# Four-layer residual network on one core: order of the LoRA spread, split float32r for a weight mix, earlier last products, a store in halves

## The reference

```python
# 0: one expert for each batch element, argmax of cond_8; H = 256
up, gate = x @ wu.T + bu, x @ wg.T + bg;  out = (silu(up) * gate) @ wd.T + bd
# 1: base weight, and LoRA of 8 experts of rank 16, mixed by cond_8
out = x @ W_base.T + b_base + 2.0 * sum_e cond[b, e] * (x @ As[e].T) @ Bs[e].T
# 2: a weight for each batch element, mixed from 8 by cond_8, masked
w_b = sum_g cond[b, g] * (weight[g] * mask);  out = x @ w_b.T + bias
# 3: top-2 of 8 gelu-gated experts with softmax weights, and a shared one; H = 512
out = sum_k w[b, k] * mlp(x, expert[b, k]) + mlp(x, shared)
```

## Time and profile before

| what | us |
|---|---|
| runs, median (3 runs) | 153.5 (153.43 to 153.65) |
| the profiled execution, its own time | 153.69 |
| its span in the profile | 151.7 |
| TensorE busy | 147.4 (97% of the span) |
| VectorE busy | 109.8 (72%) |
| ScalarE busy | 72.0 (47%) |
| GpSimd busy | 91.4 (60%) |

### The profile page before, as it was taken

One profiled execution on the slowest core, in us unless ns is written; L12 is line 12 of the kernel. 1 busy time (PEld: TensorE's weight loads), 2 busy tenths in 40 slices (PEclk: granted clock), 3 DMA queues, 4 the chain that ended last, 5 costly groups with the idle time before them and its releaser, 6 DMA issues.

```text
span 151.7 us, 3108 instructions
## 1 busy us (share of the span) xinstructions
PE 147.4 (97%) x1075; PEld 135.1 (89%) x1075; DVE 109.8 (72%) x229; ACT 72.0 (47%) x138; POOL 91.4 (60%) x93
## 2 busy tenths in 40 slices
PE   7999999999999999999999999999999999999992
PEld 2479999999978999999989999999999999999881
DVE  3985666667996586867775967876587895968772
ACT  2875444461375554454444354545425434345640
POOL 1003999999700007849994939995876999880000
PEclk9999999999999999999999999999999999999999
DMA  2999999974354676393397386095447047000052
GB/s 62 414 401 403 411 405 394 420 298 144 154 190 138 175 160 225 78 302 109 78 309 252 130 269 215 0 300 206 190 134 280 4 139 274 4 4 0 0 209 72
DMA packets 13912, 30.15 MB, mean 199 GB/s; under 512 B 1337, under 2 KB 8009, under 8 KB 13769
## 3 DMA queue, kind: packets, MB, share of 16 engines
q1 hardware_dynamic: 13472, 28.76, 54.7%
q10 hardware_dynamic: 424, 1.20, 2.0%
HBM read 24.71 MB, written 1.05 MB: 170 GB/s over the span
## 4 chain that ended last, share of the span: by engine, by line
PE 89%; DVE 4%; POOL 3%; ACT 2%; issue 1%; ACTq 0%; DVEq 0%; POOLq 0%
PE pair L550 22%; PE pair L540 12%; PE acc L599 10%; PE pair L482 10%; PE pair L557 8%; PE acc L584 6%; PE acc L608 5%; PE acc L490 5%; PE acc L438 2%; PE pair L526 2%; PE pair L497 2%; POOL duo_lo L372 2%; PE pair L471 2%; PE pair L445 2%; DVE hid L771 2%; ACT hid_hi L431 2%
## 5 line engine op out<-in xcount | busy, mean ns | idle before, releaser
L372 POOL TENSOR_TENSOR duo_lo<-raw_duo,duo_hi 128x512 fp32r<-128x512 f32 x36 | 48.6, 1350 | 2.9
L762 DVE TENSOR_TENSOR hid_lo<-hid,hid_hi 128x512 fp32r<-128x512 f32 (+1 forms) x41 | 36.1, 882 | 17.8 <-ACT hid_hi L431 17.3
L431 ACT ACTIVATE hid_hi<-hid 128x512 fp32r<-128x512 f32 (+1 forms) x41 | 25.4, 621 | 44.0 <-DVE hid L771 41.1
L369 POOL CAST duo_hi<-raw_duo 128x512 fp32r<-128x512 f32 x36 | 28.3, 786 | 28.5 <-PE acc L599 28.5
L771 DVE TENSOR_TENSOR hid<-pair,act 128x512 f32<-128x512 f32 (+1 forms) x49 | 32.9, 673 | 5.7 <-PE pair L550 4.2
L550 PE MATMUL pair<-x_duo,duo_hi 128*128 128x256 f32 x192 | 35.2, 281 | 0.2 <-POOL duo_lo L372 0.2
L412 ACT ACTIVATE act<-pair 128x512 f32<-128x512 f32 x48 | 28.3, 590 | 9.7 <-PE pair L550 7.7
L550 PEld LDWEIGHTS pair<-x_duo,duo_hi 128*128 128x128 f32 x192 | 29.7, 189 | 0.8 <-issue 0.3
L550 PE MATMUL pair<-x_duo,duo_lo 128*128 128x256 f32 x96 | 26.9, 280 | 0.0
L540 PE MATMUL pair<-x_hl,shared_hi 128*128 128x512 f32 x64 | 20.5, 401 | 0.1
L550 PEld LDWEIGHTS pair<-x_duo,duo_lo 128*128 128x128 f32 x96 | 18.0, 188 | 0.0
(11 more groups left out here) (101 smaller groups left out, 199.2 us busy)
## 6 DMA issues: line engine op xcount, KB each, us to landing
raw_duo<-experts SPq DMA_DIRECT2D x12, 768.0 KB, 5.2
ring<-experts SPq DMA_DIRECT2D x16, 386.5 KB, 6.7
raw_solo<-experts SPq DMA_DIRECT2D x8, 768.0 KB, 5.3
x_duo<-x_hl SPq DMA_DIRECT2D x24, 128.0 KB, 4.0
x<-xT ACTq DMA_DIRECT2D x1, 1024.0 KB, 6.2
lora_raw<-x SPq DMA_DIRECT2D x4, 256.0 KB, 2.4
raw_solo<-shared SPq DMA_DIRECT2D x1, 768.0 KB, 9.8
out<-lora_raw SPq DMA_DIRECT2D x3, 256.0 KB, 2.8
```

The costliest lines, as they stand in the source:

```text
L369: pool.tensor_copy(duo_hi[:, j % HALVES, piece(n)], raw_duo[:, j % RAWS, piece(n)])\
L372: pool.tensor_tensor(duo_lo[:, j % HALVES, piece(n)], raw_duo[:, j % RAWS, piece(n)], duo_hi[:, j % HALVES, piece(n)].bitcast(F32), ALU.su ...
L431: act.activation(hid_hi[:, k % SPLITS, at], hid3[:, u % PAIRS, at], ACT.Copy)\
L762: dve.tensor_tensor(hid_lo[:, k % SPLITS, at], hid3[:, u % PAIRS, at], hid_hi[:, k % SPLITS, at].bitcast(F32), ALU.subtract).then_inc(hid_ ...
```

## The change

It does five things. SyncE loads `lora_sb` ahead of `cond_sb`. VectorE makes the first piece of `bs_w` ahead of the copy of `at_row`, which in turn stands ahead of `onehot` and `chosen_b`; TensorE makes `prepare1(0)` ahead of the rank products, and two warming products in a row instead of one and two. Layer 2's weight mix is made in float32r from split operands: GpSimd splits `w2_sb` into `w2_hi` and `w2_lo`, two experts at a time, VectorE splits `y_delta` into `y_hi` and `y_lo` right behind it, and TensorE makes three float32r products where there was one in float32; the split parts use buffers that layer 3 needs later. `gateup(47)` is put right behind `gateup(46)`, ahead of `down(44)`. The last store is cut into partitions 0 to 63 on SyncE's queue and 64 to 127 on ScalarE's.

```diff
--- before.py
+++ after.py
@@ -79,6 +79,8 @@
     ORDER += _di[0:2] + _si[0:1] + _ri[0:1] + _di[2:4] + _si[1:2] + _di[4:6] + _ri[1:2] + _si[2:3]
 ORDER += _d[18:20] + _r[6:7] + _d[20:22] + _r[7:8] + _d[22:24] + _s[12:16]
 UNITS = len(ORDER)
+
+LAST = slice(B * P - N2, B * P)
 AT = {unit: n for n, unit in enumerate(ORDER)}
 SPLIT_AT = {unit: n for n, unit in enumerate(x for x in ORDER if x[0] != "R")}
 ENDS = [x for x in ORDER if x[0] == "R" or (x[0] == "D" and x[2] == 1)]
@@ -183,6 +185,9 @@
         lora_raw = sb("lora_raw", [P, B, P])
         x_sum = lora_raw[:, :, :].rearrange("p b n -> p (b n)")
         lin1 = sb("lin1", [P, B, P])
+        w2_hi = duo_hi[:, 0, 0:E * P].rearrange("p (k n) -> p k n", k=E)
+        w2_lo = duo_lo[:, 0, 0:E * P].rearrange("p (k n) -> p k n", k=E)
+        y_hi, y_lo = x_duo[:, 0, 0, :], x_duo[:, 0, 1, :]
         mix_raw = sb("mix_raw", [P, E, B, R])
         lin2 = sb("lin2", [P, B, P])
 
@@ -216,6 +221,8 @@
         chosen_done, rank_mm, payload_done, slots_mm, slots_done = (
             sem("chosen_done"), sem("rank_mm"), sem("payload_done"), sem("slots_mm"), sem("slots_done"))
         ydelta_done, bsw_done = sem("ydelta_done"), sem("bsw_done")
+        yhi_done, ylo_done, w2_hi_done, w2_lo_done = (
+            sem("yhi_done"), sem("ylo_done"), sem("w2_hi_done"), sem("w2_lo_done"))
         prep_mm, prep_copied = sem("prep_mm"), sem("prep_copied")
         lin2_done, lin1_done = sem("lin2_done"), sem("lin1_done")
         shared_hi_done, shared_done = sem("shared_hi_done"), sem("shared_done")
@@ -251,8 +258,8 @@
 
         @block.sync
         def _(sp):
+            sp.dma_start(lora_sb[:, :], lora).then_inc(lora_in, 16)
             sp.dma_start(cond_sb[:, :], cond).then_inc(cond_in, 16)
-            sp.dma_start(lora_sb[:, :], lora).then_inc(lora_in, 16)
             sp.dma_start(w2_sb[:, :, :], w2).then_inc(w2_in, 16)
 
             def load0(b):
@@ -327,11 +334,12 @@
             sp.wait_ge(x_summed, SUMMED[ORDER[-1]] - 2)
             for g in range(G - 1):
                 sp.dma_start(out[:, group(g)], x_sum[:, group(g)]).then_inc(stored, 16)
-            for n in range(2):
-                at = slice((G - 1) * N + n * N2, (G - 1) * N + (n + 1) * N2)
-                sp.wait_ge(x_summed, SUMMED[ORDER[-1]] - 1 + n)
-                sp.dma_start(out[:, at], x_sum[:, at]).then_inc(stored, 16)
-            sp.wait_ge(stored, 16 * (G + 1))
+            at = slice((G - 1) * N, (G - 1) * N + N2)
+            sp.wait_ge(x_summed, SUMMED[ORDER[-1]] - 1)
+            sp.dma_start(out[:, at], x_sum[:, at]).then_inc(stored, 16)
+            sp.wait_ge(x_summed, SUMMED[ORDER[-1]])
+            sp.dma_start(out[0:P // 2, LAST], x_sum[0:P // 2, LAST]).then_inc(stored, 16)
+            sp.wait_ge(stored, 16 * (G + 2))
 
         @block.gpsimd
         def _(pool):
@@ -339,6 +347,14 @@
             pool.memset(ones[:, :], 1.0).then_inc(ones_set, 1)
             pool.wait_ge(cond_in, 16)
             pool.tensor_copy(earlier_b[:, :], cond_sb[:, EARLIER:EARLIER + B]).then_inc(ones_set, 1)
+
+            pool.wait_ge(w2_in, 16)
+            for n in range(E // 2):
+                at = slice(2 * n, 2 * n + 2)
+                pool.tensor_copy(w2_hi[:, at, :], w2_sb[:, at, :]).then_inc(w2_hi_done, 1)
+                pool.wait_ge(w2_hi_done, n + 1)
+                pool.tensor_tensor(w2_lo[:, at, :], w2_sb[:, at, :], w2_hi[:, at, :].bitcast(F32), ALU.subtract)\
+                    .then_inc(w2_lo_done, 1)
 
             pool.wait_ge(small_in, 16)
             pool.wait_ge(slots_done, 1)
@@ -431,6 +447,9 @@
                         act.activation(hid_hi[:, k % SPLITS, at], hid3[:, u % PAIRS, at], ACT.Copy)\
                            .then_inc(hid_hi_done, 1)
 
+            act.wait_ge(x_summed, SUMMED[ORDER[-1]])
+            act.dma_start(out[P // 2:P, LAST], x_sum[P // 2:P, LAST]).then_inc(stored, 16)
+
         @block.tensor
         def _(pe):
             def warm(times):
@@ -452,24 +471,25 @@
             pe.wait_ge(ones_set, 3)
             pe.wait_ge(at_diag_done, 1)
             pe.matmul(acc[1][:, 0:B], ones_b[:, :], at_diag[:, :], start=True, stop=True).then_inc(at_mm, 1)
-            warm(1)
+            warm(2)
+            prepare1(0)
 
             pe.wait_ge(chosen_done, 1)
             pe.matmul(pair[2][0][0:B, 0:E], earlier_b[:, :], chosen_b[:, :], start=True, stop=True)
             pe.matmul(pair[2][0][0:B, E:2 * E], ones_b[:, 0:B], chosen_b[:, :], start=True, stop=True)\
               .then_inc(rank_mm, 1)
-            warm(2)
-            for q in range(G):
+            for q in range(1, G):
                 prepare1(q)
 
-            pe.wait_ge(ydelta_done, 1)
-            pe.wait_ge(w2_in, 16)
+            pe.wait_ge(ylo_done, 1)
             for k in range(E):
                 n = G + k // 2
                 if k % 2 == 0:
                     pe.wait_ge(prep_copied, n - len(prep) + 1)
-                ins = pe.matmul(prep[n % 3][:, (k % 2) * B * R:(k % 2 + 1) * B * R], w2_sb[:, k, :],
-                                y_delta[:, :, :].rearrange("p b j -> p (b j)"), start=True, stop=True)
+                    pe.wait_ge(w2_lo_done, k // 2 + 1)
+                for m, (w, y) in enumerate(((w2_hi, y_hi), (w2_hi, y_lo), (w2_lo, y_hi))):
+                    ins = pe.matmul(prep[n % 3][:, (k % 2) * B * R:(k % 2 + 1) * B * R], w[:, k, :], y,
+                                    start=(m == 0), stop=(m == 2))
                 if k % 2 == 1:
                     ins.then_inc(prep_mm, 1)
 
@@ -617,8 +637,11 @@
             gateup(1)
             pe.wait_ge(lin_read, 2 * G)
             for u in range(UNITS):
-                if u + AHEAD < UNITS:
+                if u + AHEAD < UNITS - 1:
                     gateup(u + AHEAD)
+                if u + AHEAD == UNITS - 2:
+
+                    gateup(UNITS - 1)
                 down(u)
 
         @block.vector
@@ -633,31 +656,40 @@
             dve.tensor_tensor(at_diag[:, :], top_at[:, 0:1].to_broadcast([B, B]), cond_sb[:, EYE:EYE + B], ALU.mult)\
                .then_inc(at_diag_done, 1)
 
-            step = [3]
-
-            def chained(ins):
-                step[0] += 1
-                ins.then_inc(route, 1)
-                dve.wait_ge(route, step[0])
-
-            chained(dve.tensor_tensor(onehot[:, :, :], top_at[:, 0:K].unsqueeze(2).to_broadcast([B, K, E]),
-                                      cond_sb[:, IOTA:IOTA + E].unsqueeze(1).to_broadcast([B, K, E]), ALU.is_equal))
-            dve.tensor_tensor(chosen_b[:, :], onehot[:, 0, :], onehot[:, 1, :], ALU.add).then_inc(chosen_done, 1)
-            dve.wait_ge(rep_in, 16)
-            dve.wait_ge(at_mm, 1)
-            dve.tensor_copy(at_row[:, :], acc[1][0:1, 0:B]).then_inc(at_done, 1)
-            dve.wait_ge(lora_in, 16)
-            for q in range(G):
+            def spread(q):
                 at = slice(q * GB, (q + 1) * GB)
                 dve.scalar_tensor_tensor(
                     bs_w[:, at, :], lora_sb[:, BS1:BS1 + P].unsqueeze(1).to_broadcast([P, GB, P]), LORA_SCALE,
                     cond_rep[:, at].unsqueeze(2).to_broadcast([P, GB, P]), ALU.mult, ALU.mult)\
                    .then_inc(bsw_done, 1)
 
+            dve.wait_ge(rep_in, 16)
+            dve.wait_ge(lora_in, 16)
+            spread(0)
+            dve.wait_ge(at_mm, 1)
+            dve.tensor_copy(at_row[:, :], acc[1][0:1, 0:B]).then_inc(at_done, 1)
+            step = [3]
+
+            def chained(ins):
+                step[0] += 1
+                ins.then_inc(route, 1)
+                dve.wait_ge(route, step[0])
+
+            chained(dve.tensor_tensor(onehot[:, :, :], top_at[:, 0:K].unsqueeze(2).to_broadcast([B, K, E]),
+                                      cond_sb[:, IOTA:IOTA + E].unsqueeze(1).to_broadcast([B, K, E]), ALU.is_equal))
+            dve.tensor_tensor(chosen_b[:, :], onehot[:, 0, :], onehot[:, 1, :], ALU.add).then_inc(chosen_done, 1)
+            for q in range(1, G):
+                spread(q)
+
             dve.wait_ge(small_in, 16)
-            dve.tensor_tensor(y_delta[:, :, :], cond_rep[:, :].unsqueeze(2).to_broadcast([P, B, R]),
-                              small_sb[:, DELTA:DELTA + R].unsqueeze(1).to_broadcast([P, B, R]), ALU.mult)\
+            delta = small_sb[:, DELTA:DELTA + R].unsqueeze(1).to_broadcast([P, B, R])
+            dve.tensor_tensor(y_delta[:, :, :], cond_rep[:, :].unsqueeze(2).to_broadcast([P, B, R]), delta, ALU.mult)\
                .then_inc(ydelta_done, 1)
+            y = y_delta[:, :, :].rearrange("p b j -> p (b j)")
+            dve.wait_ge(ydelta_done, 1)
+            dve.tensor_copy(y_hi, y).then_inc(yhi_done, 1)
+            dve.wait_ge(yhi_done, 1)
+            dve.tensor_tensor(y_lo, y, y_hi.bitcast(F32), ALU.subtract).then_inc(ylo_done, 1)
 
             dve.wait_ge(exp_done, 1)
             chained(dve.reciprocal(inv[:, 0:1], expsum[:, :]))
```

(8 more changed lines are left out.)

5 lines of the change are left out of this document (removed).

## The result

Four runs have a median of **157.35 us** (157.26 to 158.75) against 153.57 us for the kernel before: a ratio of **1.0262**, 95% interval 1.0202 to 1.0323. The forecast was 156.0 us in a range up to 157.2: the sign was right, the size was too small, and the median lies 0.15 us outside the range. (Ratios pair runs of one chip and leave disturbed runs out, so they can differ a little from the quotient of two medians.)

The account below looks back on a forecast made before the run. TensorE bounds the kernel, with VectorE's payload chain setting the head: 153.69 + 2.55 (later slots' product) − 0.05 (last unit) = 156.2, median 0.19 below, so 156.0 us; range 153.9 to 157.2.

Parts of the forecast that it names:

- TensorE has no slack, and the head's delay reaches the end: Whole kernel: TensorE busy 147.4 of 151.7 us, so what the head gains or loses arrives at the end.
- Turns, for 16 partitions too: Head: VectorE's narrow two-operand instructions also wait out GpSimd's; payload at 15.2 to 15.3, L506 2.55 us later; chance 0.60.
- the second rival: Head: only wide instructions take turns with GpSimd; L506 1.65 us later, 155.1 us in all; chance 0.13.
- The first turn: Head: VectorE's `spread(3)` waits for GpSimd's first cast and ends at 6.7 us, ahead of `y_delta`.
- `y_hi` and `y_lo`, 0.75: VectorE's chain in the head: the new copy and subtraction add 0.75 us, between 0.5 and 0.9.
- `cond`, 0.5: Start of VectorE's chain: `cond`, second in the queue, delays all that hangs on it 0.5 us, at most some 0.8.
- TensorE would be at `upgate0(0)` near 11.1: Head: with all inputs ready TensorE reaches `upgate0(0)` near 11.1 instead of 11.94; float32r products save 0.65 us.
- The store, taken as 0: Tail: storing the last piece in halves costs 0 us, between −0.2 and +0.4.
- 0.4 in a rival: Tail: store halves go one behind the other at half rate, 0.9 us instead of 0.45; chance 0.25 within any case.
- The last unit, 0.05: Tail: `gateup(47)` ahead of `down(44)` gains 0.05 us most likely, nothing at least, 0.35 at most.
- The clock falling behind the idle stretch: Layer 0: 2 us idle ahead of L506 drops the clock to 1.2 GHz, making 156.9 us; chance 0.1 within case of turns.
- Layer 3: Layer 3, after the head: the prediction had no term for a change in time here.

Follow-up runs that it names:

- the kernel with the filled gap: Kernel before with the `lora` and `cond` loads exchanged and seven instead of five warming products at the start: 154.63 us, ratio 1.005.

## Why the prediction was right in sign and too small

- **TensorE has no slack, and the head's delay reaches the end.** Right: 3.07 at the slots' product, 3.05 at 44 us, 3.60 in the span.
- **Turns, for 16 partitions too** (the forecast against the second rival). Right. Forecast: 2.1 of the 3.2 by which the payload is late; measured 1.79 alone, 1.88 of the 2.64 with the split of `y`, and in the changed kernel, by difference, 2.2 of 3.75. That 2.1 and 2.2 are so near is partly luck. The first turn, 0.75 before `y_delta`, did not take place: GpSimd's first cast waited for VectorE instead. The turns behind `y_lo` cost some 0.8 more in its place: GpSimd's last subtraction ended at 11.94 and not at 10.9, so `pw_all` ended as forecast (11.13 against 11.1), but `reached` had still to wait, 0.72 long instead of 0.28. And of the scalings that read one tensor, `pw_rest` did not pass freely.
- **`y_hi` and `y_lo`, 0.75.** Measured 0.76.
- **`cond`, 0.5.** This term was mis-sized: 0.94 on the chain, since the transfer itself took 2.2 instead of 1.7. The payload ended at 15.77, not 15.2 to 15.3. It is the failed step of the sum on the chain's side: 0.44 of the 0.5 us by which the slots' product was later than forecast, and with it of the 1.2 us that the profiled time was above the 156.2 of the sum; the other 0.1 is in the turns. The 0.44 is read from the rows and not isolated: with `cond` first the payload comes only 0.35 earlier, as `spread(0)` then waits for `lora`.
- **"TensorE would be at `upgate0(0)` near 11.1"; everything else on `cond` just 0.5 later.** Wrong by 2.9. `prepare1` started at 5.19 instead of 4.7, 0.5 later; it and the rank products ran to 10.79, 5.6 us instead of 3.6, 2.0 more for records at half the pace; the float32r products took 3.2 instead of 2.8, 0.4. In this kernel it cost almost nothing, as the payload was later still, and left 0.78 of idle time where over 2 were forecast; it made most of the 1.6 us in the kernel with the swap alone, and it is why undoing the split alone does not help. The prediction read "full clock throughout" from the earlier trace rows, where the paces of single instructions would have said otherwise: the five warming products of before took 2.31 us, 0.46 each, and two of the same in the kernel with the filled gap 0.54, 0.27 each. No rival held it.
- **The store, taken as 0, with 0.4 in a rival.** The rival was right: 0.34. That is 0.3 of the 1.2, and the second failed step. The prediction says that the 0.4 enters the range, but its upper end, 156.5 and most of a unit at the lower clock, has no term for it; with it the median would have lain inside. That issuing takes the same whatever the size was not in the earlier trace rows either: a half took 0.56, the whole 0.43.
- **The last unit, 0.05.** Measured 0.04, the tail's wait still 0.3.
- **The clock falling behind the idle stretch** (fifth case, chance 0.1). Its sign, a mean clock of 0.989, is there in one of the four runs, 158.75, and in 16 of the 40 runs with such a stretch: likelier than said, but the median is not from it.
- **Layer 3**, at nothing: 0.25 longer. At 90 us a down product waits for an addition of VectorE's, which ends at 90.78 (87.40 before) and stands behind a `hid_lo` that takes its turn with GpSimd in both kernels, 1.78 us long after and 1.61 before. The chain of both:

```profile
90.93 0.95 PE acc L619 x6
```

```profile
87.76 0.74 PE acc L599 x6
```

  0.95 against 0.74 for the same six records. That such meetings fall otherwise once the head has shifted is what the rows suggest; no run tests it, and the prediction had no term for it. It is the third failed step, 0.25 of the 1.2.

0.5 for the chain, 0.34 for the store, 0.25 in layer 3 and 0.13 outside the span make the 1.2 us. That the median came out only 0.15 above the range is owed to the room left there for a clock that did not fall.

## What to carry to other kernels

A swap of two loads is not priced by the queue slot: follow the small one's landing, then everything idle until it lands, and ask what pace the engine has afterwards. Work given to an idle GpSimd beside a chain of small VectorE instructions cost this chain the rest of a GpSimd instruction at most meetings, though it was 16 partitions wide. Where undoing one part brings nothing, undo two: delays that run side by side hide each other.

## What the runs showed that was not expected

- VectorE instructions of one or two elements in 16 partitions took 0.69 to 0.73 us beside a GpSimd subtraction of 128x256 and 0.15 or 0.16 when alone, one with a single tensor input (`pw_rest`) among them.
- A GpSimd cast started at 5.65 let VectorE's last `spread`s and `y_delta`, one behind another, go first (1.84 us for one of 0.4): the turns are not strict.
- With 0.9 us without work for TensorE early in the run, its next four to six float32 records took twice as long, while the clock row, which has no record that early, shows full; two more warming products in that gap made the kernel with the swapped loads 1.1 us faster.
- Idle stretches as short as 0.7 to 2 us ahead of the slots' product were followed, in 16 of 40 runs, by a lower mean clock; the two profiles that caught it show one stretch at 1.2 GHz behind them (0.56 and 0.64 of the full clock from 15.20 to 18.60).
- A 10 KB load behind one of 128 KB on the same queue landed 2.2 to 3.1 us after its issue, 1.6 to 1.8 ahead of it.
